# Three projections of batch 1, from the first pass to the stretch ahead of it

## Chip, cores and metric

The kernel runs on one core of a Trainium2 chip. The metric is the device time in microseconds (us) of one execution. Before the change it is 773.31 us, the median of three runs (773.23, 773.31, 774.62).

## What is computed

A transformer block on x of shape (4, 512, 512): four batches, 512 positions, width 512; 32 query heads and 8 key and value heads of 16 features, hidden width 1376.

```
x = x + attention(layernorm(x), Wq, Wk, Wv, Wo)
x = x + ffn(layernorm(x), W_gate, W_up, W_down)
# attention
q, k, v = h @ Wq, h @ Wk, h @ Wv
q = q * cos + rotate_half(q) * sin
k = k * cos + rotate_half(k) * sin
att = where(causal, q @ k.T / sqrt(16), -inf)
out = (softmax(att) @ v) @ Wo
# ffn
(silu(h @ W_gate.T) * (h @ W_up.T)) @ W_down.T
```

## The kernel before

The program has two phases. `phase_1` does the attention of all batches up to the weighted values and the output projection of batch 0; `phase_2` does the rest. The change is in `phase_1` alone.

**The stretch in front.** TensorE transposes the normalised x of batch 0 (four units), makes its key projection (R0), its four query projections (R1 to R4) and its values (V, U), and transposes x of batch 1 (T0 to T3). A unit is a result of one PSUM bank. An R or V unit is 12 matmuls of 512 columns: four chunks of the contraction times three products of high and low parts; they are issued in four pieces of three (`project`, L1124). Then come the scores of groups 0 and 1 of batch 0. A group is one key head with its four query heads. Its scores fill 11 banks of `ps_s` (three in rotation), and VectorE takes the row maximum of each bank (`row_max`: L921 for groups 0 and 1, L916 after). ScalarE and VectorE split the maxima of group 0 in two, TensorE transposes them (`transposed_max`, L1190), ScalarE copies the result to `m_t` (L776), and SyncE stages it as two more rows of `q_rows`.

**The passes.** Four passes (`iteration(b)`, b = 0 to 3) of 8 groups with 4 slots each, 32 slots. In a slot of group n TensorE makes transposed scores of n (`ps_t`, L1206), scores of n + 2 (L1172) and weighted values of n or n - 1 (`ps_o`, L1219). ScalarE takes the exponential (L786), GpSimd masks it (`mask_probs`, L685 and L687), VectorE takes the maxima of group n + 2. At the start of each group GpSimd splits the maxima of the next one (`split_max`, L676 and L678), and TensorE transposes them after the fourth score of the group.

**The projections of the next batch** lie between these. A pass has 40 gaps, five to a group, at the places (slot, head) (0,1), (0,3), (1,3), (2,1), (2,3). `QKV_UNITS` gives each unit's first gap; R and V take one piece in each of four gaps, U and T all four pieces in one:

```
QKV_UNITS = [("R", 0, 0), ("R", 1, 5), ("R", 2, 10), ("R", 3, 15), ("R", 4, 20), ("V", 0, 25), ("U", 0, 30)]
NEXT_T = [("T", 0, 32), ("T", 1, 34), ("T", 2, 36), ("T", 3, 38)]
ROPE_SLOT = [3, 4, 5, 6, 7, 8, 11, 11, 12, 12, 13, 14, 16, 17, 19, 20, 21, 22, 23, 24]
LO_SLOT = {7: 0, 14: 1, 15: 2, 22: 3, 25: 4}
```

All of a pass's units use the one bank `ps_d`. ScalarE copies R units out to `raw` (`raw_rows`, L737; for keys also two half copies, L723 and L724). GpSimd turns them by position in 20 steps (`rotate`, L589; a remainder, L593, in five of them, each followed by `rotated_low`, L604), step s in slot `ROPE_SLOT[s]`. ScalarE takes the top parts (`rotated_top`, L747), and SyncE writes the parts to memory (`store_rotated`) one slot after `LO_SLOT`. T units are transposes of the batch after next (L1113); ScalarE and VectorE (`xt_low`, L895) read them. VectorE also does the layer norm of that batch in passes 0 and 1 (`STATS_AT`, `APPLY_AT`). Pass 2 has no T units; in pass 3 the W units are the output projection of batch 0, and its T units transpose batch 0 for the second phase (`last_xt`).

## Time and profile before

| | |
|---|---|
| median of three runs | 773.31 us |
| profiled execution | 775.21 us |
| its span, first to last instruction | 773.5 us |
| TensorE busy | 742.8 us, 96% |
| VectorE busy | 433.9 us, 56% |
| ScalarE busy | 334.7 us, 43% |
| GpSimd busy | 240.8 us, 31% |
| TensorE's mean granted clock | 0.987 of full speed |

Times inside the execution are counted from the span's start. Busy time is the union of an engine's instructions; a matmul's record also covers its way through the array, so the start-to-start distance of two neighbours is what one costs in a stream. A granted clock of 1.00 is 2.4 GHz, 0.50 is 1.2 GHz. The row ends with the idle time in front of an instruction, and with what ended it.

### The profile page before, as it was taken

Reading aid. Unit: us, or ns where it says so; the run is one execution under the profiler, and the core shown is the slowest. Engines: PE = TensorE matmul, PEld = TensorE weight load, DVE = VectorE, ACT = ScalarE, POOL = GpSimd, SP = SyncE. Lnnn points to the kernel's source line nnn. Section 1 sums busy time; section 2 is a strip of 40 time slices with the busy share of each in tenths; the row PEclk is TensorE's granted clock in tenths of the full one; section 3 lists DMA queues with packets and bytes.
Section 4 is the critical chain, followed back from the end, with each engine's and each line's share of the span. In section 5 each row is a group of like instructions: output and inputs, shape, how many; then the busy total and the mean of one; then the engine's idle time right before and its main releaser. Section 6 shows DMA issues by size and latency. Waiting matters only on the chain.

```text
span 773.5 us, 12217 instructions
## 1 busy us (share of the span) xinstructions
PE 742.8 (96%) x4180; PEld 505.5 (65%) x4180; DVE 433.9 (56%) x1120; ACT 334.7 (43%) x646; POOL 240.8 (31%) x467
## 2 busy tenths in 40 slices
PE   5899999999999999998999999999999999999998
PEld 4645444554454543443788888888888888788886
DVE  6898788887877778997354443233232233231212
ACT  3337767766876788677343222111121111121111
POOL 4157785678557874555000000000000000000000
PEclk9869999999999999999999999999999999999999
DMA  7337677233434454530592102311004020020001
GB/s 271 97 108 254 216 250 228 66 100 111 120 94 126 149 171 148 165 98 36 168 311 69 42 14 107 94 59 54 15 35 156 27 81 27 0 108 1 1 0 55
DMA packets 74759, 81.86 MB, mean 106 GB/s; under 512 B 8864, under 2 KB 58528, under 8 KB 74496
## 3 DMA queue, kind: packets, MB, share of 16 engines
q1 hardware_dynamic: 73408, 79.98, 32.5%
q10 hardware_dynamic: 1296, 1.18, 0.5%
q8 instruction: 30, 0.49, 0.3%
q14 instruction: 25, 0.20, 0.1%
HBM read 57.02 MB, written 33.36 MB: 117 GB/s over the span
## 4 chain that ended last, share of the span: by engine, by line
PE 51%; DVE 0%; issue 0%; DVEq 0%
PE bank L1562 35%; PE ps_y L1614 15%; PE bank L1601 1%; DVE x_in L1544 0%; DVEq L1543 0%
## 5 line engine op out<-in xcount | busy, mean ns | idle before, releaser
L916 DVE CUSTOM_DVE_ANT_0 ps_s<-ps_s,mask_row 128x512 f32<-128x512 f32 (+1 forms) x360 | 192.8, 583 | 50.8 <-PE ps_s L1172 48.0
L786 ACT ACTIVATE probs<-ps_t 128x512 f32<-128x512 f32 (+1 forms) x352 | 179.3, 559 | 70.0 <-PE ps_t L1206 69.9
L1519 DVE TENSOR_TENSOR h<-h,bank 128x512 f32<-128x512 f32 (+1 forms) x44 | 30.2, 687 | 217.2 <-PE bank L1562 217.2
L1172 PE MATMUL ps_s<-k_rows,q_rows 96*128 96x256 bf16 (+3 forms) x512 | 140.5, 309 | 3.5 <-DVE m_raw L916 1.5
L1206 PE MATMUL ps_t<-q_rows,k_rows 98*128 98x512 bf16 (+1 forms) x352 | 127.1, 365 | 3.4 <-ACT probs L786 2.1
L238 POOL TENSOR_TENSOR var_eps<-mean_var,eps 128x1 f32<-128x1 f32 x16 | 3.0, 189 | 282.5 <-DVE mean_var L233 282.5
L1457 ACT ACTIVATE h<-bank 128x512 f32<-128x512 f32 (+1 forms) x44 | 26.3, 598 | 147.5 <-PE bank L1562 147.5
L687 POOL TENSOR_SCALAR_AFFINE_SELECT probs<-probs 128x512 f32<-128x512 f32 x128 | 83.2, 650 | 0.0
L1463 ACT CAST h_hi<-h 128x512 fp32r<-128x512 f32 (+1 forms) x44 | 27.3, 620 | 128.4 <-DVE h L1519 128.4
L1219 PE MATMUL ps_o<-probs,v_ones 128*32 128x512 f32 (+3 forms) x1024 | 82.0, 439 | 0.2 <-ACT o_sb L796 0.2
L1172 PEld LDWEIGHTS ps_s<-k_rows,q_rows 96*128 96x128 bf16 x512 | 49.3, 100 | 43.1 <-DVE m_raw L916 13.8
L1206 PEld LDWEIGHTS ps_t<-q_rows,k_rows 98*128 98x128 bf16 x352 | 34.3, 98 | 52.9 <-issue 20.7
L1614 PE MATMUL ps_y<-wd_hi,h_hi 128*128 128x512 f32 (+1 forms) x176 | 68.8, 391 | 0.0
L1614 PE MATMUL ps_y<-wd_lo,h_hi 128*128 128x512 f32 (+1 forms) x176 | 68.6, 390 | 0.0
L1614 PE MATMUL ps_y<-wd_hi,h_lo 128*128 128x512 f32 (+1 forms) x176 | 68.6, 390 | 0.0
L685 POOL TENSOR_TENSOR carrier<-half 128x1 f32<-128x1 f32 x128 | 26.9, 210 | 95.8 <-ACT probs L786 95.6
L1219 PEld LDWEIGHTS ps_o<-probs,v_ones 128*32 128x32 f32 x1024 | 27.0, 109 | 42.7 <-issue 32.9
L916 DVE DVE_READ_ACCUMULATOR2_ANT m_raw<- 128x1 f32 x360 | 50.5, 140 | 0.0
L1562 PE MATMUL bank<-xt_hi,wg_hi 128*128 128x512 f32 (+1 forms) x128 | 50.0, 390 | 0.0
L1562 PE MATMUL bank<-xt_hi,wg_lo 128*128 128x512 f32 (+1 forms) x128 | 49.9, 390 | 0.0
L1562 PE MATMUL bank<-xt_hi,wu_lo 128*128 128x512 f32 (+1 forms) x128 | 49.9, 390 | 0.0
L1562 PE MATMUL bank<-xt_lo,wg_hi 128*128 128x512 f32 (+1 forms) x128 | 49.9, 390 | 0.0
(161 smaller groups left out, 1370.8 us busy)
## 6 DMA issues: line engine op xcount, KB each, us to landing
scratch_o<-o_sb SPq DMA_DIRECT2D x31, 256.0 KB, 2.1
q_rows<-scratch_q_parts SPq DMA_DIRECT2D x32, 192.0 KB
x_in<-in_x SPq DMA_DIRECT2D x16, 256.0 KB, 4.5
q_rows<-scratch_q_parts SPq DMA_DIRECT2D x32, 128.0 KB
o_in<-scratch_o SPq DMA_DIRECT2D x64, 64.0 KB
inverse<-scratch_inverse SPq DMA_DIRECT2D x64, 64.0 KB
x_res<-in_x SPq DMA_DIRECT2D x16, 256.0 KB, 2.8
out<-x_in SPq DMA_DIRECT2D x16, 256.0 KB, 2.0
```

What stands on the lines that cost most here:

```text
L685: nc.gpsimd.tensor_tensor(carrier[:, g % 2, c:c + 1], half[:, 0:1], half[:, 0:1], ALU.add)
L687: nc.gpsimd.affine_select(out=diagonal, in_=diagonal, compare_op=ALU.is_ge, fill=0.0, base=0, pattern=[[0, GROUP], [1, P]], channel_multip ...
L786: nc.scalar.activation(probs[:, g % 2, heads * u:heads * (u + 1), CHUNK_AT[c]:CHUNK_AT[c + 1]], ps_t[:, pos % S_BANKS, 0:heads * CHUNK_N[c ...
L916: taken = nc.vector.tensor_tensor_reduce(out=head, in0=head, in1=mask_row[:, T - width:T], scale=1.0, scalar=LOWEST, op0=ALU.add, op1=ALU. ...
L1172: mm = nc.tensor.matmul(bank[:, place], q_rows[r][0:ROWS, j, P * q:P * (q + 1)], k_rows[r][0:ROWS, 0:width], start=(place == 0), stop=(mas ...
L1206: nc.tensor.matmul(ps_t[:, pos % S_BANKS, 0:heads * width], k_rows[r][:, P * c:P * (c + 1)], q_rows[r][:, heads * u:heads * (u + 1), P * c:T],
L1219: mm = nc.tensor.matmul(ps_o[32 * j:32 * j + 2 * DH, P * c:T], v_ones[:, c, g % NKV, :], probs[:, g % 2, j, CHUNK_AT[c]:CHUNK_AT[c + 1]], ...
L1457: nc.scalar.activation(h[0:m, r], bank[units["gate", f] % BANKS][0:m, :], ACT.Silu).then_inc(silu_done, 1)
L1463: nc.scalar.copy(h_parts[0][0:m, r], h[0:m, r]).then_inc(h_hi_ready, 1)
L1519: nc.vector.tensor_tensor(h[0:m, r], h[0:m, r], bank[units["up", f] % BANKS][0:m, :], ALU.mult).then_inc(h_ready, 1)
L1562: mm = nc.tensor.matmul(out, weights(w, c), moving(m, c), start=(c == 0 and n == 0), stop=(c == chunks - 1 and n == 2))
L1614: mm = nc.tensor.matmul(ps_y[:, t], h_parts[w][0:m, r, P * t:P * (t + 1)], wd[p][0:m, f, :], start=(f == 0 and k == 0), stop=(f == FT - 1 ...
```

## The change

- Units R0, R1 and R2 of batch 1 (`AHEAD` = 3) leave pass 0. Their 12 pieces stand between the scores of groups 0 and 1 (`AHEAD_AT`: group, slot, head, to unit and piece), R0 into `ps_t`, R1 into `ps_d`, R2 into `ps_o`. The transposed maximum of group 0 goes to a bank of `ps_t` and has semaphores of its own.
- ScalarE copies R0 out ahead of `rotated_top(0, 4)` and of the first maximum, and R1 and R2 behind the last store of batch 0. GpSimd does rotation steps 0 to 2 of batch 1 ahead of pass 0.
- Pass 0 has R3, R4, V and U at gaps 5, 12, 18 and 23; its rotation steps 3 to 19 stand in slots 0 to 19 (`FIRST_ROPE`), and its stores in slots 3, 8, 11, 18 and 22.
- In passes 1 and 2 R2 to U start one gap earlier. In passes 0 and 1 T0 does too. In `ROPE_SLOT` of these passes steps 8 and 11, both with a remainder, no longer share group 3's slots (12 to 15); `MEAN_SLOT` is 15, so that GpSimd's part of the layer norm stands in slot 16, which is group 4's.
- In pass 3 units T1 to T3 go to the three banks of `ps_s` and no longer to `ps_d`.

The declaration of the two new semaphores (`first_max_ready`, `first_max_evacuated`) and unchanged lines are left out:

```diff
@@ -70,29 +70,37 @@
-QKV_UNITS = [("R", 0, 0), ("R", 1, 5), ("R", 2, 10), ("R", 3, 15), ("R", 4, 20), ("V", 0, 25), ("U", 0, 30)]
-NEXT_T = [("T", 0, 32), ("T", 1, 34), ("T", 2, 36), ("T", 3, 38)]
+QKV_UNITS = [("R", 0, 0), ("R", 1, 5), ("R", 2, 9), ("R", 3, 14), ("R", 4, 19), ("V", 0, 24), ("U", 0, 29)]
+NEXT_T = [("T", 0, 31), ("T", 1, 34), ("T", 2, 36), ("T", 3, 38)]
...
               ("T", 3, 39)]
-UNITS_IN = [QKV_UNITS + NEXT_T] * (B - 2) + [QKV_UNITS, LAST_UNITS]
-PRE_DENSE = KC + N_ROPE + 2 + KC
-PRE_UNITS = PRE_DENSE + 1
...
+AHEAD = 3
+AHEAD_AT = {(0, 1, 1): (0, 0), (0, 1, 3): (0, 1), (0, 2, 1): (0, 2), (0, 2, 3): (0, 3),
+            (1, 0, 1): (1, 0), (1, 0, 3): (1, 1), (1, 1, 1): (1, 2), (1, 1, 3): (1, 3),
+            (1, 2, 1): (2, 0), (1, 2, 3): (2, 1), (1, 3, 1): (2, 2), (1, 3, 3): (2, 3)}
+FIRST_UNITS = [("R", 3, 5), ("R", 4, 12), ("V", 0, 18), ("U", 0, 23)]
+UNITS_IN = [FIRST_UNITS + NEXT_T] + [QKV_UNITS + NEXT_T] * (B - 3) + [QKV_UNITS, LAST_UNITS]
+PRE_DENSE = KC + N_ROPE + 2 + KC + AHEAD
 PRE_BANKS = 1 + S_BANKS
-UNIT0 = [PRE_UNITS + sum(len(u) for u in UNITS_IN[:b]) for b in range(B)]
...
-ROPE_SLOT = [3, 4, 5, 6, 7, 8, 11, 11, 12, 12, 13, 14, 16, 17, 19, 20, 21, 22, 23, 24]
+UNIT0 = [PRE_DENSE + sum(len(u) for u in UNITS_IN[:b]) for b in range(B)]
...
+ROPE_AHEAD = 3
+FIRST_ROPE = [None] * ROPE_AHEAD + [0, 1, 2, 3, 4, 5, 6, 7, 8, 9, 10, 13, 14, 15, 17, 18, 19]
+ROPE_SLOT = [FIRST_ROPE] + [[3, 4, 5, 6, 7, 8, 10, 10, 11, 12, 13, 14, 15, 17, 18, 19, 21, 22, 23, 25]] * (B - 2)
...
 PRE_STEPS = PAIR_STEPS
-LO_SLOT = {7: 0, 14: 1, 15: 2, 22: 3, 25: 4}
-NEXT_XT = {26: 0, 27: 1, 29: 2, 31: 3}
+LO_SLOT = [{2: 0, 7: 1, 10: 2, 17: 3, 21: 4}] + [{7: 0, 13: 1, 16: 2, 23: 3, 27: 4}] * (B - 2)
+NEXT_XT = {25: 0, 27: 1, 29: 2, 31: 3}
...
-X_SLOT, MEAN_SLOT = 26, 14
+X_SLOT, MEAN_SLOT = 26, 15
@@ -305,10 +313,16 @@
+        LAST_UNIT0 = UNIT0[B - 1]
...
-            if isinstance(unit, int) and unit < PRE_DENSE and unit % PRE_BANKS:
+            if unit == PRE_DENSE - 1:
+                return ps_o[:]
+            if unit < PRE_DENSE and unit % PRE_BANKS:
                 return ps_t[:, unit % PRE_BANKS - 1]
+            if unit > LAST_UNIT0 + TT:
+                return ps_s[:, unit - LAST_UNIT0 - TT - 1]
@@ -374,9 +389,17 @@
+        def v_unit(b):
...
+            return UNIT0[b - 1] + len(UNITS_IN[b - 1]) - KC - 1 if 0 < b < B - 1 else UNIT0[b] - 1 if b else KC + N_ROPE + 1
...
-            return UNIT0[b - 1] + k if b else KC + k
+            if b == 0:
+                return KC + k
+            if b == 1:
+                return PRE_DENSE - AHEAD + k
+            return UNIT0[b - 1] + k
@@ -453,7 +476,7 @@
                 if n == 0:
-                    sp.wait_ge(dense_evacuated, PRE_UNITS)
+                    sp.wait_ge(first_max_evacuated, 1)
@@ -513,8 +536,8 @@
                         load_x(b + 3)
-                    if has_next and slot - 1 in LO_SLOT:
-                        store_rotated(sp, b + 1, LO_SLOT[slot - 1])
+                    if has_next and slot - 1 in LO_SLOT[b]:
+                        store_rotated(sp, b + 1, LO_SLOT[b][slot - 1])
@@ -668,6 +691,8 @@
                     rotated_low(0, REST_STEP.index(s))
+            for s in range(ROPE_AHEAD):
+                rotate(1, s)
@@ -700,7 +725,7 @@
                     if has_next:
-                        for s, at in enumerate(ROPE_SLOT):
+                        for s, at in enumerate(ROPE_SLOT[b]):
@@ -772,8 +797,8 @@
                 if n == 0:
-                    act.wait_ge(dense_ready, PRE_UNITS)
-                    nc.scalar.copy(m_t[0][:], ps_d[rows, 0:P]).then_inc(dense_evacuated, 1)
+                    act.wait_ge(first_max_ready, 1)
+                    nc.scalar.copy(m_t[0][:], ps_t[rows, 0, 0:P]).then_inc(first_max_evacuated, 1)
@@ -821,14 +846,14 @@
                         if g == 0:
-                            v_place(b, UNIT0[b - 1] + 6 if b else KC + N_ROPE + 1)
+                            v_place(b, v_unit(b))
...
                                 dense_read(b, *done[slot, j])
-                    if has_next and slot in LO_SLOT:
-                        rotated_top(b + 1, LO_SLOT[slot])
+                    if has_next and slot in LO_SLOT[b]:
+                        rotated_top(b + 1, LO_SLOT[b][slot])
@@ -864,10 +889,13 @@
             store_rotated(act, 0, 3)
+            raw_rows(1, 0, r_unit(1, 0))
...
             store_rotated(act, 0, 4)
+            for k in range(1, AHEAD):
+                raw_rows(1, k, r_unit(1, k))
@@ -983,7 +1011,7 @@
                     if slot in NEXT_XT:
-                        work.append(lambda: xt_low(b + 2, NEXT_XT[slot], UNIT0[b] + len(QKV_UNITS) + NEXT_XT[slot]))
+                        work.append(lambda: xt_low(b + 2, NEXT_XT[slot], UNIT0[b + 1] - KC + NEXT_XT[slot]))
@@ -1102,6 +1130,9 @@
+                if piece == 0 and unit > LAST_UNIT0 + TT:
+                    pe.wait_ge(max_done, BANKS_OF * GROUPS)
+                    return
@@ -1182,8 +1213,8 @@
                 if n == 0:
-                    bank_free(PRE_UNITS - 1, 0)
-                    to, ready = ps_d[:], dense_ready
+                    pe.wait_ge(dense_evacuated, KC + N_ROPE + 2 + KC)
+                    to, ready = ps_t[:, 0], first_max_ready
@@ -1199,6 +1230,8 @@
                 pos = T_AT[c] + u
+                if n == 0 and c == 0 and j == 0:
+                    pe.wait_ge(dense_evacuated, PRE_DENSE - AHEAD + 1)
@@ -1211,7 +1244,9 @@
                 if c == 0:
-                    if positive(n):
+                    if n == 0:
+                        pe.wait_ge(dense_evacuated, PRE_DENSE)
+                    else:
@@ -1251,7 +1286,7 @@
                         mm.then_inc(dense_ready, 1)
-            for unit in range(KC, PRE_DENSE):
+            for unit in range(KC, PRE_DENSE - AHEAD):
@@ -1263,6 +1298,9 @@
                         scores(0, n, i, j)
+                        if (n, i, j) in AHEAD_AT:
+                            k, piece = AHEAD_AT[n, i, j]
+                            dense(1, "R", k, r_unit(1, k), piece)
```

TensorE's queue at the end of group 1's first slot, before. `ps_s` holds scores, `m_parts` the split maxima of group 0; the row with 384 columns opens the second slot.

```order
113 L1172 MATMUL ps_s<-k_rows,q_rows 128x512
114 L1179 MATMUL ps_s<-mask_q,ident_b 128x128
115 L1190 MATMUL ps_d<-ident_b,m_parts 128x128
116 L1172 MATMUL ps_s<-k_rows,q_rows 128x384
117 L1179 MATMUL ps_s<-mask_q,ident_b 128x128
118 L1172 MATMUL ps_s<-k_rows,q_rows 128x384
```

And with the change (`xt`, `w`: parts of batch 1's x and of the weights):

```order
126 L1203 MATMUL ps_s<-k_rows,q_rows 128x512
127 L1210 MATMUL ps_s<-mask_q,ident_b 128x128
128 L1203 MATMUL ps_s<-k_rows,q_rows 128x512
129 L1210 MATMUL ps_s<-mask_q,ident_b 128x128
130 L1155 MATMUL ps_d<-xt_hi,w_hi 128x512
131 L1155 MATMUL ps_d<-xt_lo,w_hi 128x512
132 L1155 MATMUL ps_d<-xt_hi,w_lo 128x512
133 L1221 MATMUL ps_t<-ident_b,m_parts 128x128
134 L1203 MATMUL ps_s<-k_rows,q_rows 128x384
135 L1210 MATMUL ps_s<-mask_q,ident_b 128x128
```

Two pieces of R1 stand in this slot, one of them just ahead of the transposed maximum, which now goes to `ps_t`. The other ten pieces stand in the same way behind each second score from group 0's second slot on.

ScalarE's queue from the last `rotated_top` of batch 0 to the first exponentials, before:

```order
24 L747 COPY r_top<-rot 128x1024
25 L767 CAST m_parts<-m_raw 128x16
26 L776 CAST m_t<-ps_d 32x128
27 L403 DMA scratch_q_parts<-r_top 16x8x512 x2
28 L403 DMA scratch_q_parts<-r_low 16x8x512
29 L786 ACTIVATE probs<-ps_t 128x512 x4
```

And with the change:

```order
24 L748 ACTIVATE raw<-ps_t 64x512
25 L749 COPY raw<-ps_t 64x512
26 L762 COPY raw<-ps_t 128x512
27 L772 COPY r_top<-rot 128x1024
28 L792 CAST m_parts<-m_raw 128x16
29 L801 CAST m_t<-ps_t 32x128
30 L426 DMA scratch_q_parts<-r_top 16x8x512 x2
31 L426 DMA scratch_q_parts<-r_low 16x8x512
32 L762 COPY raw<-ps_d 128x512
33 L762 COPY raw<-ps_o 128x512
34 L811 ACTIVATE probs<-ps_t 128x512 x4
```

Three copies of R0 (`raw<-ps_t`) now precede the last `r_top` and the first maximum (`m_parts`, `m_t`), and two copies, of R1 and R2, precede the first exponentials of pass 0.

GpSimd's queue in pass 0, from the first split of maxima to the fourth mask, before (`carrier` and AFFINE_SELECT are one mask; `rot` and `turned` are rotation steps):

```order
35 L676 CAST m_parts<-m_raw 128x16
36 L678 TENSOR_TENSOR m_parts<-m_raw,m_parts 128x16
37 L685 TENSOR_TENSOR carrier<-half 128x1
38 L687 AFFINE_SELECT probs<-probs 128x4x128
39 L685 TENSOR_TENSOR carrier<-half 128x1
40 L687 AFFINE_SELECT probs<-probs 128x4x128
41 L685 TENSOR_TENSOR carrier<-half 128x1
42 L687 AFFINE_SELECT probs<-probs 128x4x128
43 L589 TENSOR_TENSOR rot<-raw,cos 128x512
44 L685 TENSOR_TENSOR carrier<-half 128x1
45 L687 AFFINE_SELECT probs<-probs 128x4x128
```

And with the change:

```order
38 L701 CAST m_parts<-m_raw 128x16
39 L703 TENSOR_TENSOR m_parts<-m_raw,m_parts 128x16
40 L616 TENSOR_TENSOR rot<-rot 128x512
41 L627 TENSOR_TENSOR r_low<-rot 128x512
42 L710 TENSOR_TENSOR carrier<-half 128x1
43 L712 AFFINE_SELECT probs<-probs 128x4x128
44 L612 TENSOR_TENSOR rot<-raw,cos 128x512
45 L710 TENSOR_TENSOR carrier<-half 128x1
46 L712 AFFINE_SELECT probs<-probs 128x4x128
47 L612 TENSOR_TENSOR rot<-raw,sin 128x512
48 L710 TENSOR_TENSOR carrier<-half 128x1
49 L712 AFFINE_SELECT probs<-probs 128x4x128
```

Before, one rotation step stands ahead of the fourth mask and none ahead of the first three. Now three steps and an `r_low` stand among the first three masks, and one more step and the fourth mask follow the last row shown.

## Rows read from the trace of the kernel before

**Rows 1.** Stretch, length, busy us (x) of PE, PEld, DVE, ACT, POOL; PEclk; DMA, GB/s.

```profile
40.50:53.60 13.10, 12.11 (x56) 5.45 (x57) 12.44 (x23) 2.46 (x4) 7.52 (x7) 0.63 0.42 122
57.04:137.55 80.51, 77.72 (x565) 39.57 (x565) 65.41 (x217) 59.76 (x121) 57.48 (x107) 1.00 0.71 230
370.76:773.50 402.74, 399.58 (x1776) 327.96 (x1776) 132.71 (x216) 82.64 (x140) 8.87 (x24) 1.00 0.21 68
```

**Rows 2.** The same view, from one transposed maximum to the next.

```profile
57.00:66.30 9.30, 9.30 (x58) 4.79 (x57) 7.27 (x26) 7.32 (x15) 4.79 (x12) 1.00 0.75 269
66.30:76.50 10.20, 10.20 (x75) 5.23 (x75) 8.49 (x28) 7.64 (x15) 10.04 (x16) 1.00 0.65 224
76.50:87.30 10.80, 10.21 (x75) 5.25 (x75) 8.43 (x28) 6.71 (x14) 6.76 (x14) 1.00 0.70 229
87.30:98.00 10.70, 10.29 (x74) 5.18 (x73) 8.09 (x31) 8.48 (x16) 10.38 (x19) 1.00 0.82 240
98.00:108.20 10.20, 10.16 (x74) 5.24 (x75) 7.71 (x26) 6.71 (x14) 8.47 (x14) 1.00 0.73 253
108.20:117.30 9.10, 9.10 (x72) 4.67 (x72) 8.24 (x26) 7.16 (x15) 8.42 (x16) 1.00 0.65 195
117.30:127.90 10.60, 9.19 (x75) 4.57 (x74) 8.48 (x28) 8.43 (x18) 5.18 (x12) 1.00 0.87 264
127.90:137.60 9.70, 9.36 (x74) 4.70 (x72) 8.80 (x30) 7.31 (x16) 3.45 (x11) 1.00 0.50 155
...
168.00:179.40 11.40, 10.36 (x74) 5.20 (x73) 8.10 (x31) 8.53 (x16) 11.08 (x19) 1.00 0.27 83
...
287.70:295.70 8.00, 7.86 (x63) 3.13 (x62) 6.96 (x26) 5.84 (x14) 3.43 (x10) 1.00 0.65 188
```

**Rows 3.** The same view, cut where TensorE's clock changed.

```profile
43.00:47.40 4.40, 4.40 (x22) 2.11 (x21) 4.24 (x9) 0.65 (x2) 4.16 (x5) 0.50 0.40 117
47.40:50.80 3.40, 2.47 (x15) 0.75 (x13) 3.24 (x7) 1.35 (x3) 1.01 (x1) 1.00 0.12 35
50.80:54.20 3.40, 3.35 (x17) 1.85 (x16) 3.24 (x7) 0.00 (x0) 0.00 (x0) 0.50 0.69 203
```

**Rows 4.** Neighbouring projection matmuls in the timeline, slow and full clock.

```profile
14.25 0.63 PE L1124 MATMUL ps_d<-xt_hi,w_lo 128*128 128x512 f32 x1
14.68 0.63 PE L1124 MATMUL ps_d<-xt_hi,w_hi 128*128 128x512 f32 x1
...
27.42 0.39 PE L1124 MATMUL ps_d<-xt_lo,w_hi 128*128 128x512 f32 x1
27.64 0.39 PE L1124 MATMUL ps_d<-xt_hi,w_lo 128*128 128x512 f32 x1
```

**Rows 5.** Timeline: TensorE's first transposed score, the start of pass 0.

```profile
53.59 0.63 PE L1206 MATMUL ps_t<-q_rows,k_rows 98*128 98x512 bf16 x1
```

**Rows 6.** Timeline, ScalarE: last top part, first maximum, a copy of `raw`.

```profile
47.33 1.04 ACT L747 COPY r_top<-rot 128x1024 bf16<-128x1024 bf16 x1 [3.75 <-POOL rot L593]
48.28 0.21 ACT L767 CAST m_parts<-m_raw 128x16 bf16<-128x16 f32 x1
60.59 0.59 ACT L723 ACTIVATE raw<-ps_d 64x512 f32<-64x512 f32 x1 [0.26 <-PE ps_d L1124]
```

**Rows 7.** Timeline, GpSimd: a rotation step, then, one mask later, a remainder.

```profile
68.12 1.28 POOL L589 TENSOR_TENSOR rot<-rot,turned 128x512 f32<-128x512 f32 x1
...
70.10 1.04 POOL L593 TENSOR_TENSOR rot<-rot 128x512 f32<-128x512 f32 x1
```

**Rows 8.** Timeline, TensorE: the waits for a transfer, GpSimd and the bank.

```profile
84.14 0.39 PE L1206 MATMUL ps_t<-q_rows,k_rows 98*128 98x512 bf16 x1 [0.59 <-DMA q_rows<-m_t]
...
122.82 0.63 PE L1113 MATMUL ps_d<-ident,xn 128*128 128x128 f32 x4 [1.16 <-DVE xt_lo L895]
...
179.44 0.23 PE L1190 MATMUL ps_t<-ident_b,m_parts 128*128 128x128 bf16 x1 [1.08 <-POOL m_parts L678]
...
365.74 0.63 PE L1113 MATMUL ps_d<-ident,xn 128*128 128x128 f32 x4 [1.17 <-DVE xt_lo L895]
```

3 lines of the change are left out of this document (2 added, 1 removed).

## Prediction

> **What bounds the kernel now.** I read the time by stages first, then the same view cut from one transposed maximum to the next, then where the clock changes, then the timeline and the order of the queues. The second phase keeps TensorE busy for 399.6 of 402.7 us [rows 1]; the change does not touch it. In pass 0 TensorE is busy for 77.7 of 80.5 us, the other engines for 57 to 65. In the stretch before it, from 40.5 to 53.6, VectorE is the full engine (12.4 of 13.1 us, 23 instructions, 0.54 each), and TensorE has a mean clock of 0.63 only. So projections leave a stretch that TensorE bounds for one that VectorE bounds. The questions are how much room there is, at which clock, and what bounds pass 0 when TensorE has less to do.
>
> **Price of a piece.** Projection matmuls follow each other by 0.22 to 0.23 us at full clock (27.42, 27.64) and by 0.43 at half clock (14.25, 14.68) [rows 4]. A piece of three is 0.68 or 1.28 us. Twelve pieces move: 8.2 or 15.3 us. The Trainium skill, in "TensorE: Matmul & The Clock Gate", section "Back-to-back issue gap", gives about 131 ns for a 512-column matmul in a stream with weight loads. By that the 36 matmuls would be 4.7 us instead of 8.2, and about 3.5 less would be moved; the rows disagree with it, and nothing below uses it.
>
> **Ahead of pass 0** (the cost). I follow the queue from the sixth bank of scores, done at about 43.6, since everything before it is unchanged. The clock is at half until 47.4 [rows 3]; I keep that.
> - To 47.4: two pieces of R0 (2.6) and most of three banks of scores (0.43 each). Then at full clock the rest of that bank, one more, and two pieces: R0 is done at 49.4.
> - ScalarE now copies R0 out first, three copies of 0.6 [rows 6], to 51.2. Behind them wait the last `r_top` (1.04, at 47.33 before) and the first maximum (at 48.28 before), which ends at 52.5 (another 0.21). VectorE stands still for about 1.6 us behind that maximum, since its low part is next in its queue; TensorE for about 0.9. The transposed maximum is out at 53.2.
> - VectorE has ten banks left, at about 0.55 each: to 58.3. TensorE has seven banks of scores (4608 columns, 1.9 us), six pieces (4.1) and 0.7 of waiting for banks: the first transposed score comes at 59.9, where it was at 53.59 [rows 5].
> - ScalarE copies R2 (0.6) before the first exponential, which TensorE meets three banks on: 0.9. On the other side the two pieces of R0 are gone from the first slot (1.36), and the clock is full, where 0.6 us were at half (0.2 saved).
> So the transposed maximum at 57.04 [rows 1] moves to about 62.0: **+5.0 us**. Bounds: with every piece at half clock and nothing hidden it is 15.3 less 1.6, so +13.7; with full clock from 43.6 on it is 3.8/2 less, and without VectorE's standstill 0.9 less, so +2.2. I take the replay, because the clock was in fact granted at 47.4, and TensorE now has more to do in that time, not less.
>
> **Pass 0** (the gain). Two windows give a rule. Four pieces in a group: 10.2 us (the second of rows 2). None: 8.0 (287.7 to 295.7). Four pieces are 2.7 us, so TensorE's own floor is 7.4 and another limit is 8.0; there VectorE is busy for 6.96. With layer norm or `xt_low` beside it VectorE is busy for 8.2 to 8.8 in 9.1 to 9.7 us. GpSimd's prices: a step 1.25, a mask 0.73 (what is left from 68.12 to 70.10) [rows 7], a remainder 1.1 and a low part 1.0 (its duration is 1.04 too), and as estimates a split 0.47 (two instructions of the size of the 0.21 in rows 6) and the layer norm's part 1.2. Group by group, now against after:
> - 0: 9.3; two pieces fewer give 7.9, but GpSimd gets three more steps and a low part (4.9 of busy time become 9.3, of which it did idle 1.1 late in the group): 8.2.
> - 1: 10.2; two pieces, 8.8; GpSimd has 9.35: 9.35.
> - 2 and 3: 10.8 and 10.7; still four pieces: 10.2 each. The transfer of the maxima came 0.59 late at 84.14 [rows 8], and GpSimd, full for 10.38 of 10.7, becomes lighter by a step and a low part.
> - 4: 10.2; no piece but U: GpSimd with 9.3 (layer norm, two steps, remainder, low part) is the limit: 9.3.
> - 5: 9.1 to 8.8; T0 is here instead of two pieces and U, and VectorE has 8.2.
> - 6: 10.6 to 9.3; the wait of 1.16 for `ps_d` at 122.82 [rows 8] goes, as T0 is a gap earlier.
> - 7: 9.7 to 9.6.
> Sum 74.95 against 80.5: **-5.6 us**. Bounds: -8.2 - 1.2 + 1.36, so -8.0, if only TensorE counted; -2.3 if groups 0 and 1 take GpSimd's 10.0 of the window at 66.3 and the others VectorE's 9.7.
>
> **Other queues in pass 0.** SyncE has six writes of the keys in slot 3, then six row loads, then the staging of the next maximum; before, this stood in slots 8 and 9 and cost the 0.59 at 84.14. I expect the same wait one or two groups earlier: nothing gained or lost. GpSimd's three early steps (3.8 us) lie beside its idle stretch ahead of pass 0 (7.5 of 13.1 busy), at no cost.
>
> **Passes 1 and 2.** Group 1 gets a fifth piece in each (+0.65), group 5 one fewer (in pass 1 T0 takes its place). In pass 1 the wait of 1.16 at T0 goes (the same place as 122.82), and so does the 1.08 at 179.44 [rows 8]: there GpSimd is busy for 11.08 of 11.4 us [rows 2], and without one low part (1.0) and the layer norm (1.2) it has 9.0 beside TensorE's 10.2. Pass 1: **-1.6**. Pass 2: 0, as group 5 gives back what group 1 takes.
>
> **Pass 3.** T3 waits 1.17 for `ps_d` at 365.74 [rows 8], with only two groups' tails behind it: last transposed score, exponential, mask, weighted values, copy. In a bank of its own it waits no longer; ScalarE is free at 365.5 for the next exponential: **-1.0** (bounds 0 and -1.2).
>
> **Sum.** +5.0 - 5.6 - 1.6 + 0 - 1.0 = -3.2 us. It is made against the span of 773.5; the same difference off the median of 773.31 gives **770.1 us** (the profiled execution itself took 775.21, 1.9 above the median). A difference of less than 0.2%, 1.55 us, is about what a measurement of this kernel cannot tell from none.
>
> **The rivals.**
> 1. *The front is cheap.* The clock is granted sooner, since TensorE no longer has holes between banks. For it: at 43.0 to 47.4 TensorE is already busy throughout [rows 3]. Against: it was so at half clock for over 3 us without a grant. At +2.5 instead of +5.0, and with 1 us more from pass 0: 766.6.
> 2. *Pass 0 is held by another engine.* GpSimd takes 10.0 in groups 0 and 1, VectorE 9.7 elsewhere, as in the lower bound above: -2.3 instead of -5.6. Then the sum is +0.1: 773.4, no change. For it: VectorE at 8.8 of 9.7 us in the eighth window of rows 2, and GpSimd's 10.04 in the second. Against: the 9.1 us window with two layer norm steps shows that VectorE can take 8.2 in 9.1.
> 3. *The front is at half clock.* At 50.8 the clock fell, after 3.4 us in which TensorE was busy for 2.47 only [rows 3]. With VectorE standing still and TensorE following it bank by bank, the clock falls again or is not granted at 47.4. Each us at half clock costs 0.5. The change loses its gain when half clock lasts 6.4 us beyond 47.4. From 47.4 to the end of the stretch TensorE has 12.5 us of work less waits of about 1.6, so nearly 11 us at full clock would be 22 at half: +11, of which waits for VectorE and ScalarE hide about 3. That gives +13.0 in front and a time of about 778. For it: rows 3, where half clock holds from 50.8 to 54.2 with TensorE busy for 3.35 of 3.4 us. Against: pieces fill just those holes. The Trainium skill's "TensorE: Matmul & The Clock Gate", section "A second HAM failure mode: psum-queue depth-cycling", describes this: short idle times between groups of matmuls that cycle through banks make the clock go up and down. By it the time would be that of this rival or between it and the forecast; the fall at 50.8 agrees with it.
>
> **How the numbers follow.** Forecast 0.49 (768.3 to 771.7), rival 1 0.14, rival 2 0.22, rival 3 with its milder forms 0.15. Rival 2 lies within 0.2% in most of its chance; of the forecast's upper edge and rival 3's mild forms a little does too. Faster by over 0.2% (under 771.76): 0.62. Within 0.2%: 0.23. Slower (over 774.86): 0.15. The range leaves out the faster half of rival 1 (under 766.0) and most of the slower cases: 766.0 to 775.5.
>
> **What would show it.** First transposed score near 60 and the transposed maximum after it near 62; TensorE's clock at full from 47.4 without another fall; the first maximum on ScalarE at 52 behind three copies and `r_top`. Pass 0 of about 75 us with groups 0, 1 and 4 at 8.2 to 9.4, GpSimd busy nearly all of groups 1 and 4, and no wait at T0 of passes 0 and 1; group 3 of pass 1 at 10.3; no wait for T3 at the end. A pass 0 of 78 us speaks for rival 2; half clock after 51 for rival 3; a first transposed score before 57.5 for rival 1. The forecast is wrong if the second phase changes its length, since nothing here prices that.

## The result and the profile after

The changed kernel takes 780.83 us, the median of four runs (779.23 to 784.76), against 773.51 for the kernel before on the same chip: a ratio of 1.0094, with a 95% interval from 1.0074 to 1.0114. It is slower by 7.3 us. The forecast said 770.1, faster; its range, 766.0 to 775.5, does not hold the result. In a second set eleven runs of the change gave 778.19 (775.33 to 782.0) against 774.45, a ratio of 1.0044 [1.0026, 1.0063]. So the loss is 4 to 7 us, and both intervals lie above 1.

The profiled execution took 779.23 us, its span is 777.5, against 773.5 before: 4.0 us to explain. I cut it as the forecast did. This is the view by stretches of the changed kernel (columns as in [rows 1]): from the sixth bank of scores to the first transposed score, pass 0, and the second phase.

```profile
40.50:62.06 21.56, 19.16 (x90) 11.25 (x92) 14.60 (x24) 4.71 (x8) 11.61 (x10) 0.82 0.29 82
64.02:143.61 79.59, 71.29 (x528) 34.26 (x535) 65.92 (x221) 57.01 (x118) 52.65 (x103) 1.00 0.73 232
376.30:777.50 401.20, 398.06 (x1776) 326.64 (x1776) 132.81 (x216) 82.45 (x140) 8.91 (x24) 1.00 0.21 68
```

The second row is the one to look at. TensorE's work in pass 0 fell from 77.7 us [rows 1] to 71.3, as the 36 matmuls are gone. The pass fell by 0.9 only: TensorE, which had 2.8 us of idle time in it, now has 8.3. The work left the pass, and idle time took its place.

| stretch | before | after | difference | forecast |
|---|---|---|---|---|
| to the transposed maximum that starts pass 0 | 57.04 | 64.02 | +6.98 | +5.0 |
| pass 0 | 80.51 | 79.59 | -0.92 | -5.6 |
| pass 1 | 81.48 | 80.20 | -1.28 | -1.6 |
| pass 2 | 76.63 | 77.57 | +0.94 | 0 |
| pass 3, from its first group on | 58.67 | 58.68 | 0.0 | 0 |
| last transposed maximum to the second phase | 16.43 | 16.24 | -0.2 | -1.0 |
| second phase | 402.74 | 401.20 | -1.5 | 0 |

**The groups of pass 0**, from one transposed maximum to the next, groups 0 to 7 (as [rows 2] before):

```profile
64.02:73.66 9.64, 8.70 (x52) 3.59 (x52) 8.33 (x31) 7.24 (x15) 8.09 (x15) 1.00 0.58 199
73.66:82.90 9.24, 8.83 (x66) 4.19 (x68) 7.12 (x24) 7.13 (x15) 9.08 (x16) 1.00 1.02 331
82.90:93.13 10.23, 10.08 (x72) 5.13 (x74) 8.49 (x28) 7.04 (x15) 7.83 (x14) 1.00 0.78 243
93.13:103.85 10.72, 10.30 (x74) 5.00 (x73) 8.28 (x32) 7.08 (x15) 8.97 (x16) 1.00 0.85 280
103.85:113.89 10.04, 7.93 (x65) 3.77 (x66) 9.52 (x28) 7.81 (x16) 8.23 (x16) 1.00 0.58 171
113.89:122.34 8.45, 7.86 (x64) 3.78 (x66) 7.40 (x26) 6.48 (x14) 3.52 (x10) 1.00 0.67 222
122.34:133.92 11.58, 8.38 (x70) 4.13 (x69) 7.99 (x28) 6.90 (x16) 3.49 (x10) 1.00 1.00 297
133.92:143.61 9.69, 9.20 (x73) 4.67 (x71) 8.79 (x30) 7.34 (x16) 3.45 (x10) 1.00 0.32 101
```

Groups 0, 4 and 6 stand out: in each TensorE is idle for about 1 to 3 us, and in group 4 neither TensorE (7.93) nor GpSimd (8.23) fills the time, but VectorE has 9.52 of 10.04. TensorE's own waits, in the timeline of the changed kernel, name what ended each:

```profile
53.06 0.23 PE L1221 MATMUL ps_t<-ident_b,m_parts 128*128 128x128 bf16 x1 [1.20 <-DVE m_parts L956]
...
73.66 0.23 PE L1221 MATMUL ps_t<-ident_b,m_parts 128*128 128x128 bf16 x1 [0.41 <-POOL m_parts L703]
...
113.89 0.23 PE L1221 MATMUL ps_t<-ident_b,m_parts 128*128 128x128 bf16 x1 [1.04 <-POOL m_parts L703]
...
131.73 0.39 PE L1239 MATMUL ps_t<-q_rows,k_rows 98*128 98x512 bf16 x1 [2.71 <-DMA q_rows<-m_t]
...
372.08 0.64 PE L1254 MATMUL ps_o<-probs,v_ones 128*32 128x512 f32 x4 [1.11 <-POOL probs L712]
```

**In front**, the queues of the other engines explain the first of them. ScalarE, VectorE and GpSimd in the timeline of the changed kernel:

```profile
48.88 0.59 ACT L748 ACTIVATE raw<-ps_t 64x512 f32<-64x512 f32 x1 [5.06 <-PE ps_t L1155]
49.50 0.58 ACT L749 COPY raw<-ps_t 64x512 f32<-64x512 f32 x1
50.10 0.59 ACT L762 COPY raw<-ps_t 128x512 f32<-128x512 f32 x1
50.59 1.05 ACT L772 COPY r_top<-rot 128x1024 bf16<-128x1024 bf16 x1
51.53 0.22 ACT L792 CAST m_parts<-m_raw 128x16 bf16<-128x16 f32 x1
...
51.79 1.22 DVE L956 TENSOR_TENSOR m_parts<-m_raw,m_parts 128x16 bf16<-128x16 f32 x1 [1.22 <-ACT m_parts L792]
...
51.71 1.26 POOL L612 TENSOR_TENSOR rot<-raw,cos 128x512 f32<-128x512 f32 x1 [3.02 <-ACT r_top L772]
```

The first maximum on ScalarE (51.53) stands behind R0's three copies and `r_top`, as foreseen. What was not foreseen is VectorE's low part of it: 16 columns wide, 0.18 us before the change (at 48.52), 1.22 now. It starts at 51.79 and ends at 53.01; GpSimd's first early rotation step runs from 51.71 to 52.97. The Trainium skill, in "SBUF — State Buffer", section "SBUF: two separate sides", says that a VectorE instruction with two operands in SBUF and a GpSimd instruction share a pair of ports that one holds for its whole length. The trace agrees: the small instruction ends 0.04 us behind the large one.

**The clock**, same view, cut where it changed in front:

```profile
45.00:51.90 6.90, 6.81 (x39) 4.06 (x39) 4.04 (x8) 2.82 (x5) 3.65 (x5) 1.00 0.20 57
51.90:53.60 1.70, 0.23 (x1) 0.10 (x1) 1.70 (x3) 0.26 (x1) 1.62 (x2) 1.00 0.00 0
53.60:55.60 2.00, 1.74 (x9) 0.92 (x10) 2.00 (x5) 0.00 (x0) 1.92 (x2) 0.91 0.35 97
55.60:58.60 3.00, 3.00 (x12) 1.99 (x11) 1.38 (x4) 0.59 (x1) 0.08 (x1) 0.50 0.73 207
```

Full speed came 2.4 us sooner than before (45.0, not 47.4 [rows 3]); behind the idle stretch of 51.9 to 53.6 the clock fell to 1.2 GHz for 3 us. The second phase is 1.5 us shorter for a like reason, which belongs to the execution and not to the change. Before, it ran at a mean of 0.52 from 371.50 to 374.80; now it does not. In the eighteen profiled executions of this document the time from the last transposed maximum to the end is either 417.3 to 417.4 us (the change's first profile) or 419.0 to 419.2 (the kernel before, and the change's second profile). First before, then after:

```profile
371.50:374.80 3.30, 3.30 (x9) 2.51 (x8) 0.82 (x2) 0.62 (x1) 0.00 (x0) 0.52 0.67 196
```

```profile
377.00:380.30 3.30, 3.30 (x17) 2.70 (x16) 0.82 (x2) 0.62 (x1) 0.00 (x0) 1.00 0.70 196
```

**The copies.** SyncE's queue ahead of the wait at 131.73, in the timeline of the changed kernel:

```profile
120.99 1.19 SPq L451 DMA_DIRECT2D scratch_wd_raw<-in_wd  x2
122.22 0.77 SPq L469 DMA_DIRECT2D k_rows<-scratch_k_parts  x1
...
125.34 0.42 SPq L472 DMA_DIRECT2D q_rows<-scratch_q_parts  x1
125.81 0.67 SPq L482 DMA_DIRECT2D q_rows<-m_t  x1
```

The 8 KB of maxima are issued at 125.81 and TensorE has them at 131.73, 5.9 us on. Ahead of them stand two copies of 688 KB, from memory to memory, of weights that only the second phase needs (twelve of these lie in pass 0, `copy_raw`), and six row loads. The DMA engines are full in that group (share 1.00); they are so in group 1 too (1.02), where no wait followed, so the share alone does not tell.

That the two copies go out together is the change's own doing. SyncE's queue at the same place before the change:

```profile
111.93 0.57 SPq L428 DMA_DIRECT2D scratch_wd_raw<-in_wd  x1
114.52 1.23 SPq L403 DMA_DIRECT2D scratch_q_parts<-r_top  x2
...
116.43 1.00 SPq L428 DMA_DIRECT2D scratch_wd_raw<-in_wd  x1
...
120.90 0.67 SPq L459 DMA_DIRECT2D q_rows<-m_t  x1
```

There the store of slot 23 stood between the two copies of group 5. The change puts it in slot 22, ahead of both: SyncE waits for its data until 117.70, and then both copies go out at 120.99, 4.8 us ahead of the maxima.

### The profile page after: what moved, and what is told of

Read it like the earlier page. It is cut to its first block, busy times and chain, and to the rows that moved or that the text cites. A ratio compares the mean times of both kernels' runs of the same rounds, so it can differ in the third digit from the quotient of the medians.

```text
span 777.5 us, 12187 instructions
## 1 busy us (share of the span) xinstructions
PE 738.6 (95%) x4149; PEld 503.6 (65%) x4180; DVE 434.9 (56%) x1120; ACT 333.1 (43%) x646; POOL 241.9 (31%) x467
## 4 chain that ended last, share of the span: by engine, by line
PE 51%; DVE 0%; issue 0%; DVEq 0%
PE bank L1600 35%; PE ps_y L1652 15%; PE bank L1639 1%; DVE x_in L1582 0%; DVEq L1581 0%
## 5 line engine op out<-in xcount | busy, mean ns | idle before, releaser
L1203 PEld LDWEIGHTS ps_s<-k_rows,q_rows 96*128 96x128 bf16 x512 | 47.3, 99 | 47.0 <-DVE m_raw L944 22.0
L1600 PE MATMUL bank<-xt_lo,wu_hi 128*128 128x512 f32 (+1 forms) x128 | 49.9, 390 | 0.0
```

Of the source, the lines that this page charges most:

```text
L1203: mm = nc.tensor.matmul(bank[:, place], q_rows[r][0:ROWS, j, P * q:P * (q + 1)], k_rows[r][0:ROWS, 0:width], start=(place == 0), stop=(mas ...
L1600: mm = nc.tensor.matmul(out, weights(w, c), moving(m, c), start=(c == 0 and n == 0), stop=(c == chunks - 1 and n == 2))
```

## The experiments

Sixteen kernels in four sets, each timed beside the kernel before on the same chip. Two single times (of e8 and e13) at nearly twice that of their neighbours are left out of ranges and ratios; they move a median by 0.04 at most. In the tables "start" is the time of the transposed maximum that begins pass 0, and ratios are to the kernel before, with the 95% interval. Starts and passes come from one profiled execution each, so read the start with the scatter of the clock in mind: the change itself has 64.0, 62.9 (the second set), and 61.2, 61.5 and 61.6 in three kernels with the same front (e11, e4, e13). In the profiled executions the clock came back to full speed in front at 40 to 47.5 us, and in some it fell again behind the first maximum.

### First set: the parts of the change

**The rest of the change without the move** (`e1_rest_alone`): kernel before, plus

```diff
-QKV_UNITS = [("R", 0, 0), ("R", 1, 5), ("R", 2, 10), ("R", 3, 15), ("R", 4, 20), ("V", 0, 25), ("U", 0, 30)]
+QKV_UNITS = [("R", 0, 0), ("R", 1, 5), ("R", 2, 9), ("R", 3, 14), ("R", 4, 19), ("V", 0, 24), ("U", 0, 29)]
...
+            if unit > UNIT0[B - 1] + TT:
+                return ps_s[:, unit - UNIT0[B - 1] - TT - 1]
```

and with it the new rotation, store and mean slots.

> The kernel before with everything of the change except the move: R0 to R2 stay in pass 0, but the units of passes 0 to 2 start a gap earlier, T0 at gap 31, the new slots of rotation steps and stores, and T1 to T3 of pass 3 in ps_s. Theory A (the whole loss comes from the move: front and pass 0): from the trace after, pass 1 gained 1.3 us and pass 2 lost 0.9, pass 3 nothing, so the time is within 1.5 us of the kernel before, 772 to 774. Theory B (the later passes carry a loss of their own, by the fifth piece of group 1, 1.2 us in each): 775 or more.

**The maximum first on ScalarE** (`e2_max_first`): the change, with

```diff
-            raw_rows(1, 0, r_unit(1, 0))
             rotated_top(0, 4)
             first_max_high()
+            raw_rows(1, 0, r_unit(1, 0))
```

> The change, but ScalarE does the last top part of batch 0 and the first maximum ahead of the three copies of R0. Theory A (the front is late because the first maximum stands behind R0's copies and then meets GpSimd's first rotation step): VectorE's m_parts takes 0.2 and not 1.2 us, the first transposed maximum comes near 51.5 instead of 53.1 and the one of group 1 near 62 instead of 64.0, 1.5 to 2.5 us faster than the change if the clock does not fall. Theory B (TensorE's twelve pieces set the length of the front, whatever the order): the one of group 1 stays within 0.5 us of 64.0.

**GpSimd's early steps behind the split** (`e3_pool_after_split`): the change, with

```diff
+            pool.wait_ge(m_split, 1)
             for s in range(ROPE_AHEAD):
```

> The change, but GpSimd starts the three early rotation steps only when VectorE has split the first maximum. Theory A (GpSimd's step that starts at 51.71 holds up VectorE's two-input instruction of 51.79): m_parts back to 0.2 us, first transposed maximum 1.0 us earlier, at about 52.0 if the clock is granted as in the trace after. Theory B (the 1.2 us have another reason, for instance the waits in the queue): m_parts still about 1.2 us.

**The last two copies in pass 1** (`e4_copies_later`): the change, with

```diff
-                    if not positive(b) and i >= 2 and g < 6:
+                    if not positive(b) and i >= 2 and g < 5:
+                        copy_raw(2 * g + i - 2)
+                    if b == 1 and i >= 2 and g == 5:
                         copy_raw(2 * g + i - 2)
```

> The change, but the last two of the twelve copies of the raw feed-forward weights (688 KB each) are made in pass 1 and not in group 5 of pass 0. Theory A (the staging of the maxima for group 7, issued at 125.81, stood behind these two copies and landed 5.9 us later): the wait of 2.71 us at 131.73 is gone or under 0.5, the distance of the transposed maxima of groups 6 and 7 falls from 11.58 to about 9.3, and the kernel is about 2 us faster than the change. Theory B (SyncE's own lateness is the cause: six row loads ahead): the wait stays above 1.5.

| | median (range) | ratio | start | pass 0 | 1 | 2 |
|---|---|---|---|---|---|---|
| before | 774.59 | | 57.0 | 80.51 | 81.48 | 76.63 |
| e1, no move | 773.62 (771.61 to 776.04) | 0.9988 [0.9971, 1.0005] | 57.5 | 80.73 | 80.29 | 78.16 |
| e2, maximum first | 776.8 (773.18 to 780.1) | 1.0024 [1.0003, 1.0044] | 58.2 | 82.46 | 80.20 | 78.11 |
| e3, GpSimd later | 777.1 (773.31 to 778.75) | 1.0026 [1.0, 1.0053] | 61.1 | 79.79 | | |
| e4, two copies later | 777.83 (774.37 to 778.82) | 1.0041 [1.0024, 1.0057] | 61.5 | 76.93 | 80.61 | 77.62 |

What follows: e1 acquits the rest. It brings pass 1 down by 1.2 and pass 2 up by 1.5, and makes no difference that can be measured. The loss comes with the move and what was done to pass 0 for it. e3 settles the small instruction: with GpSimd held back it takes 0.18 again. VectorE and TensorE in the timeline of e3:

```profile
51.45 0.18 DVE L957 TENSOR_TENSOR m_parts<-m_raw,m_parts 128x16 bf16<-128x16 f32 x1 [1.21 <-ACT m_parts L793]
```

```profile
51.69 0.23 PE L1222 MATMUL ps_t<-ident_b,m_parts 128*128 128x128 bf16 x1 [0.15 <-DVE m_parts L957]
```

TensorE's wait fell from 1.20 to 0.15. In the ratio (1.0026, where the change has 1.0094 and, below, 1.0044) little of that can be told from scatter. e4 removed the wait of 2.7 us altogether (pass 0 at 76.93), and its ratio is 1.0041. e2 made the maximum early, but in its pass 0 the clock fell (0.96 over the pass) and the transfer came 2.67 us late. Each repair works at its place, and none of the three kernels gets under the kernel before, so the next step was to combine them.

### Second set: the change again, two repairs, and the slots

> The change itself once more, beside the variants of this call, so that they can be compared on one chip. Theory A (the time of the change scatters because TensorE's clock is granted and taken back at another point of the front and of pass 0 in each execution): 3 to 9 us slower than the kernel before, with the transposed maximum of group 1 anywhere from 61 to 66 us, and with the distances of the maxima in passes 1 to 3 the same to 0.1 us. Theory B (the 7.3 us of the first comparison are a fixed cost): within 1 us of +7.

`e6_order_copies` is e2 and e4 together.

> The change with both repairs: last top part and first maximum of batch 0 ahead of R0's copies on ScalarE, and the last two raw weight copies in pass 1. If the two losses add: m_parts 0.2 us, the transposed maximum of group 1 at 58 to 61.5, no wait over 1 us for the staged maxima in pass 0, pass 0 at about 77 us; 3 to 5 us faster than the change beside it, within 2 us of the kernel before. If they hide each other: as the better of the two alone.

`e7_slots` is e6 with GpSimd's plan of pass 0 mended and the gaps, slots and stores of pass 2 as before the change:

```diff
-FIRST_ROPE = [None] * ROPE_AHEAD + [0, 1, 2, 3, 4, 5, 6, 7, 8, 9, 10, 13, 14, 15, 17, 18, 19]
+FIRST_ROPE = [None] * ROPE_AHEAD + [0, 1, 2, 3, 4, 5, 6, 7, 8, 9, 10, 13, 14, 15, 16, 17, 20]
-LO_SLOT = [{2: 0, 7: 1, 10: 2, 17: 3, 21: 4}] + ...
+LO_SLOT = [{1: 0, 7: 1, 10: 2, 17: 3, 22: 4}] + ...
```

> As e6_order_copies, and the slots of GpSimd in pass 0 moved: the top part of the keys in slot 1, steps 17 and 18 in slots 16 and 17, step 19 and its low part in slot 20, and pass 2 with the gaps, slots and stores of the kernel before. Theory A (VectorE's normalising instructions of slots 18 and 19 take 1.3 and 1.4 instead of 0.54 us because a rotation step of GpSimd runs beside them; GpSimd is late at the end of group 4; the fifth piece costs pass 2 0.9 us): the two back near 0.54, the distance at group 4 from 10.04 to 9.2 or less, group 0 from 9.65 to 9.3 or less, pass 2 from 77.6 back to 76.6; 1.5 to 2.5 us faster than e6_order_copies. Theory B (group 4 is bound by something else): 10.0 stays.

`e8_pieces_left_out` is the change without 35 of the 36 matmuls in front: of units R0 to R2 of batch 1 only the last product is computed, so queries and keys of that batch are incomplete.

```diff
+                    if ahead and not (c == KC - 1 and n == 2):
+                        continue
```

> The change with 35 of the 36 matmuls ahead of pass 0 left out: of R0, R1 and R2 of batch 1 only the last product is computed, so keys and the first two query parts of batch 1 are wrong; everything behind them on the other engines stays. It measures what the pieces themselves cost in front. Theory A (they are paid nearly in full, since the room beside VectorE is at half clock): first transposed score at 54 to 55.5 instead of 59 to 62, 5 us or more off the change. Theory B (the order on ScalarE and the wait of VectorE make the front long, the pieces hide in it): first transposed score at 57 or later.

| | median (range) | ratio | start | pass 0 | 1 | 2 |
|---|---|---|---|---|---|---|
| before | 774.45 | | | | | |
| e5, the change | 778.19 (775.33 to 782.0) | 1.0044 [1.0026, 1.0063] | 62.9 | 80.77 | 80.25 | 78.01 |
| e6, order and two copies | 774.97 (772.68 to 776.94) | 1.0009 [0.9994, 1.0024] | 58.8 | 78.47 | 80.25 | 77.97 |
| e7, and slots | 772.62 (769.87 to 776.8) | 0.9978 [0.9962, 0.9995] | 58.7 | 78.93 | 80.81 | 76.25 |
| e8, no pieces in front | 775.11 (771.85 to 776.48) | 1.0001 [0.9983, 1.0019] | 58.8 | 80.1 | | |

e8 is the plainest statement on the change: with 35 matmuls not done at all it is still no faster than the kernel before. Leaving them out takes 3.1 us off the median. The rest is the queues and what the clock makes of them: in e8's trace TensorE waits 1.56 for VectorE's low part of the first maximum, and then runs at 1.2 GHz from about 51 to 57.5, and the maxima come 1.87 late at 127.06. e7 is the first kernel below the one before, and its group 4 takes 8.12 instead of 10.04. But its pass 0 is no shorter than e6's: two waits for the maxima's transfer, 1.77 at 76.54 and 2.03 at 116.91, and a fall of the clock behind the first (group 2 takes 11.58 at a mean of 0.87) had taken the place of what the slots won.

### Third set: the copies, and a control

`e9_all_copies_later` is e7 with all twelve copies in pass 1:

```diff
-                    if not positive(b) and i >= 2 and g < 5:
-                        copy_raw(2 * g + i - 2)
-                    if b == 1 and i >= 2 and g == 5:
+                    if b == 1 and i >= 2 and g < 6:
                         copy_raw(2 * g + i - 2)
```

> The kernel with both repairs of ScalarE's order, GpSimd's slots in pass 0 and the old pass 2 (772.62 us, pass 0 78.93) kept its two waits of 1.77 and 2.03 us for the transfer of the maxima, in groups 1 and 5 of pass 0. Now all twelve copies of the second phase's weights stand in pass 1, none in pass 0. Theory A (the 8 KB transfer is late behind the 688 KB copies): both waits fall under 0.6, pass 0 takes 75.5 to 76.5 and the time is 770 to 771. Theory B (it is late behind the stores of the keys and the row loads, which are a slot earlier here): the waits stay over 1.5, and the time is 772.6 again. Pass 1, whose DMA share was half that of pass 0, should stay at 80.2 to 80.8; if it grows by over 1 us, the copies only took the waits along.

`e10_repairs_no_move` is e1 with the same edit and pass 2 as before.

> The control for the kernel beside it: the projections stay in pass 0, and it has the rest of the change, the old pass 2 and all twelve copies in pass 1. Theory A (moving the projections is worth something once order and slots are right): 771.8 to 773, at least 1 us above the kernel with the move; from 774.5: pass 1 -1.2, the end -0.2, the wait of 0.6 in pass 0 at most. Theory B (all that is won lies in the repairs): the same as the kernel with the move or below it. Front as before (57.0 to 57.5), pass 0 80 to 80.5, pass 1 80.3, pass 2 76.6.

`e11_slots_alone` is the change with e7's two lines of slots.

> The change with GpSimd's plan of pass 0 alone repaired (last two steps and the remainder out of the slots of the layer norm's normalising, the keys' top parts a slot earlier); ScalarE's order in front, the copies and pass 2 as in the change, 778.2. Theory A (group 4 of pass 0 was held by GpSimd and by VectorE slowed beside it): group 4 falls from 10.0 to about 8.2, of which the wait for the maxima's transfer behind it takes part back; pass 0 78 to 79, time 776.3 to 777. Theory B (what a group gives the next one takes back): group 4 falls, the pass stays at 79.6 to 80.8 and the time at 778.2.

`e12_before_copies_later` is the kernel before with the edit of the copies.

> The kernel before with all twelve copies in pass 1 and nothing else. Only one wait of 0.59 for the maxima's transfer stood in pass 0 there. Theory A: it goes, 774.0 to 774.4, not to be told from the kernel before. Theory B (the copies also cost pass 0 in ways that show no wait): 773 or less. If pass 1 has less room than its DMA share suggests, it is slower than before, over 775.

| | median (range) | ratio | start | pass 0 | 1 | 2 |
|---|---|---|---|---|---|---|
| before | 774.41 | | | | | |
| e9, all three repairs | 769.4 (768.51 to 771.04) | 0.9941 [0.9927, 0.9956] | 57.7 | 73.88 | 82.40 | 76.77 |
| e10, the control | 772.13 (769.59 to 773.92) | 0.9971 [0.9958, 0.9983] | 56.6 | 79.41 | 81.63 | 76.70 |
| e11, slots alone | 777.6 (775.26 to 780.22) | 1.0037 [1.0022, 1.0051] | 61.2 | 81.55 | 80.18 | 77.48 |
| e12, before, copies later | 774.06 (770.64 to 776.41) | 0.9992 [0.9974, 1.001] | 55.2 | 80.52 | 81.47 | 76.59 |

This set answers the question. Pass 0 of e9, and groups 0, 4 and 6 of it, in the view by stretches:

```profile
57.72:131.60 73.88, 71.09 (x528) 34.01 (x535) 64.06 (x221) 56.76 (x118) 52.78 (x103) 1.00 0.45 136
```

```profile
57.72:66.78 9.06, 8.54 (x52) 3.58 (x52) 7.85 (x30) 7.09 (x15) 8.97 (x15) 1.00 0.52 160
...
96.89:105.01 8.12, 7.77 (x66) 3.78 (x66) 7.12 (x26) 7.32 (x16) 6.30 (x14) 1.00 0.26 82
...
113.12:121.92 8.80, 8.31 (x70) 4.08 (x69) 7.99 (x28) 6.89 (x16) 3.48 (x10) 1.00 0.65 196
```

TensorE's work is what it was in the change (71.09 against 71.29), and the pass is 5.7 us shorter. The move is worth 2.7 us once nothing else in pass 0 is late: e9 against the control, 769.4 against 772.13, with intervals of the ratios that do not touch. In e11 group 4 fell to 8.12, and the pass grew all the same. TensorE's waits in e11:

```profile
79.81 0.61 PE L1239 MATMUL ps_t<-q_rows,k_rows 98*128 98x512 bf16 x1 [2.50 <-DMA q_rows<-m_t]
...
122.03 0.39 PE L1239 MATMUL ps_t<-q_rows,k_rows 98*128 98x512 bf16 x1 [2.24 <-DMA q_rows<-m_t]
```

It is the same wait at two other places. The wait of 2.71 in group 6 is gone (8.80 instead of 11.58) though no copy was moved: the mended slots put the store back between group 5's two copies, which go out at 118.08 and 121.13. But the pairs at 69.06 and 112.04 now stand 5.6 and 4.9 us ahead of a staging for which a shorter group leaves less time, and behind the first wait the clock fell (means of 0.87 and 0.85 in groups 1 and 2). Before the change the copies cost nothing that can be measured: e12 without them in pass 0 has 774.06, as the first theory had it, but keeps its wait of 0.59, at 82.29, so that wait was never theirs, which neither theory had. e9 also shows a first limit: in pass 1 two copies are issued at 179.31, 1.3 us behind a staging at 178.04, and TensorE waits at 182.91. SyncE and TensorE in the timeline of e9:

```profile
178.04 0.74 SPq L484 DMA_DIRECT2D q_rows<-m_t  x1
178.82 0.44 SPq L490 DMA_DIRECT2D scratch_o<-o_sb  x1
179.31 1.22 SPq L453 DMA_DIRECT2D scratch_wd_raw<-in_wd  x2
```

```profile
182.91 0.39 PE L1241 MATMUL ps_t<-q_rows,k_rows 98*128 98x512 bf16 x1 [1.72 <-DMA q_rows<-m_t]
```

Another pair was issued 6.9 us ahead of that staging, at 171.11. The expectation had named a pass 1 longer by over 1 us as the sign that the copies only take their waits along, and in part they do: against e7, pass 0 is 5.05 shorter (waits of 1.8 and 2.0 and 1.0 of clock) and pass 1 1.6 longer.

Over all eighteen traces, where TensorE waited for the maxima, the time from their issue to TensorE's start goes by what was issued ahead. It is 2.0 to 3.3 us where no copy stands within 8 us ahead, and the pair 1.2 us behind adds nothing there (2.91 before the change, 2.98 without copies in e12). It is 3.6 to 4.0 with one copy 4.1 to 4.5 us ahead, and 4.5 to 5.9 with a pair 4.7 to 5.6 ahead. With a pair 6.7 to 7.8 us ahead it is 3.3 to 4.9.

### Fourth set: one repair taken back at a time

`e13_change_all_copies` is the change with e9's edit of the copies.

> The change with all twelve copies of the second phase's weights in pass 1, nothing else. Theory A (three causes that hide each other, of which the late transfer is one): its wait of 2.7 in group 5 goes and none takes its place in pass 0, but group 4 stays at 10.0: pass 0 76.5 to 77.5, time 774.5 to 776 against 778.2 for the change. Theory B (the copies are the cause): 771 to 773.

`e14_old_order` is e9 with ScalarE's order of the change (the edit of e2 undone).

> The repaired version (769.4) with ScalarE's order of the change in front: three copies of R0 ahead of the keys' last top part and the first maximum. Theory A (the order costs a delay of 3 us to the first transposed maximum, an idle stretch on TensorE and a fall of the clock behind it): mark of group 1 at 61 to 63 where it was 57.7, time 772.5 to 774. Theory B (VectorE's row of banks hides it, the front is bound by the clock alone): 769.4 to 770.5.

`e15_old_slots` is e9 with the two lines of e7's diff undone.

> The repaired version with GpSimd's slots of pass 0 as in the change. Theory A: group 4 back at 10.0 from 8.1, and some of it taken back by group 5; pass 0 75.3 to 76, time 770.8 to 771.5. Theory B (GpSimd's late end of group 4 is made up for in the next groups): 769.4 to 770.

`e16_copies_apart` is e9 with the copies one to a group:

```diff
-                    if b == 1 and i >= 2 and g < 6:
-                        copy_raw(2 * g + i - 2)
+                    if b == 1 and i == 2:
+                        copy_raw(g)
+                    if b == 0 and i == 2 and g >= 4:
+                        copy_raw(g + 4)
```

> The repaired version with one copy of 688 KB in the third slot of a group and none behind it: eight in pass 1, four in groups 4 to 7 of pass 0, where it had two back to back in six groups of pass 1. Theory A (two copies back to back, 1.4 MB, are what the 8 KB transfer is late behind): the wait of 1.72 in group 4 of pass 1 falls under 0.6, none over 0.6 comes up in pass 0, pass 1 80.2 to 80.8, pass 0 as it was, 73.9 to 74.2; time 767.7 to 768.5. Theory B (a single copy delays it enough, or the rows' loads do): the wait stays near 1.7 or moves to pass 0; 769.4 or more.

| | median (range) | ratio | start | pass 0 | 1 | 2 |
|---|---|---|---|---|---|---|
| before | 774.7 | | | | | |
| e13, the change, all copies later | 776.71 (772.68 to 778.18) | 1.0024 [1.0007, 1.004] | 61.6 | 79.02 | 81.28 | 77.97 |
| e14, e9 with the old order | 772.0 (770.42 to 773.94) | 0.9968 [0.9956, 0.998] | 60.4 | 73.94 | 80.88 | 76.64 |
| e15, e9 with the old slots | 771.83 (769.94 to 773.81) | 0.9969 [0.9956, 0.9981] | 59.9 | 76.57 | 80.76 | 76.72 |
| e16, e9 with copies apart | 768.37 (765.52 to 769.89) | 0.9923 [0.9903, 0.9943] | 58.6 | 74.32 | 80.26 | 76.44 |

With the two others mended, ScalarE's order costs 2.6 us (772.0 less 769.4), the slots 2.4 (771.83 less 769.4) and ten of the twelve copies 3.2 (e7's 772.62 less 769.4). By the ratios, which set each kernel against the one before on its own chip, they are 2.1, 2.2 and 2.9. With about 1.3 that pass 2 gains by its old plan (77.5 to 78.2 against 76.3 to 76.8) that is 9.5, or 8.5 by ratios, against a distance of 8.8, or 8.0, between the change (778.19) and e9. So the prices nearly add up when they are taken from the mended kernel. Taken from the change (the 778.19 of the second set), the same repairs brought 0.6 (e11), 1.5 (e13) and 1.4 (e2). The intervals allow each of these differences an error of 1.5 to 2 us, so the times alone do not separate the two sums. The traces do: in e11 and e2 a wait that goes is replaced by the next one, or by a fall of the clock. I had expected e13 to show 76.5 to 77.5 for pass 0 and 774.5 to 776 us; it has 79.02 and 776.71, because group 5 takes 10.74 where e15, with the same slots, has 8.25. The view by stretches of that group tells why, e13 first, then e15:

```profile
111.39:122.13 10.74, 10.74 (x65) 4.86 (x66) 7.57 (x26) 6.82 (x14) 3.57 (x10) 0.70 0.27 81
```

```profile
109.72:117.97 8.25, 8.01 (x65) 3.73 (x66) 7.40 (x26) 6.48 (x14) 3.51 (x10) 1.00 0.33 98
```

TensorE's mean clock is 0.70 in e13, at 1.2 GHz from 112 to about 117, behind group 4 with its two waits of 0.85 and 1.04; in e15 the same two waits cost no clock. So a group in which TensorE idles can cost a second time, in some executions.

e14 shows that the order costs time without any fall behind it. The stretch in which TensorE stands still, and what follows it, in e14:

```profile
49.85:51.55 1.70, 0.23 (x1) 0.10 (x1) 1.70 (x3) 0.26 (x1) 1.62 (x2) 1.00 0.00 0
...
52.00:60.40 8.40, 8.20 (x45) 4.76 (x44) 6.05 (x14) 2.31 (x5) 3.11 (x6) 1.00 0.37 107
```

The first row is the change's row of 51.90 to 53.60 to the last digit, 2.05 us earlier. Yet here the clock did not fall behind it, and there it did. The start is 2.7 us later than e9's, but not all of that is the order: in e14 the clock was at half for 6.8 us in front (33.4 to 40.2), in e9 for 3.4 (39.7 to 43.1). Against e2, e6 and e7, whose clock went as in e14 and whose order is e9's (58.2 to 58.8), it is 1.5 to 2.2 later. In the change's profiled execution the fall comes on top: 3 us at half clock, 1.5 at most.

e16 is the fastest here, 6.3 us or 0.8% under the kernel before, though its interval overlaps e9's. Its pass 1 has no wait for the maxima (80.26): one copy stands at 172.48, 6.2 us ahead of the staging (178.68), and one follows at 180.13. With pairs at these places the same wait was 1.72 in e9, 0.58 in e14 and 0.20 in e15, so how long they delay the 8 KB varies. A single copy is not free either: in its pass 0, with one 4.1 us ahead, the maxima come 0.33 late at 112.27, and group 5 takes 8.50 instead of 8.11.

Other expectations that were missed: pass 0 of e6 (78.47 for 77, as its group 5 ran at a mean clock of 0.82), of e11 (81.55 for 78 to 79) and of e15 (76.57 for 75.3 to 76; its time, 771.83, for 770.8 to 771.5); pass 1 of e10 (81.63 for 80.3, with waits of 0.60 and 0.74 for the maxima); e14's start (60.4 for 61 to 63) and time (772.0 for 772.5 to 774). e9 did better than expected (pass 0 73.88 for 75.5 to 76.5, time 769.4 for 770 to 771).

## Why the prediction was wrong

The step that failed is **pass 0**, -5.6 forecast and -0.9 measured. Group by group, forecast, the change, and e9:

| group | 0 | 1 | 2 | 3 | 4 | 5 | 6 | 7 | sum |
|---|---|---|---|---|---|---|---|---|---|
| forecast | 8.2 | 9.35 | 10.2 | 10.2 | 9.3 | 8.8 | 9.3 | 9.6 | 74.95 |
| change | 9.64 | 9.24 | 10.23 | 10.72 | 10.04 | 8.45 | 11.58 | 9.69 | 79.59 |
| e9 | 9.06 | 8.81 | 10.58 | 10.72 | 8.12 | 8.11 | 8.80 | 9.68 | 73.88 |

- *Other queues in pass 0, "nothing gained or lost".* This is the largest error. I priced the transfer of the maxima by the one wait of 0.59 in the trace of before and let it stand. The wait that I looked for, one or two groups earlier, did not come; another did, in group 6. Half of the 4.6 us missing in pass 0 is group 6 (2.3), which is that transfer. The rows had the warning: a DMA share of 0.87 in the group from 117.30 [rows 2], which I was about to shorten by TensorE's wait of 1.16. In e1, where that wait is gone and the projections stay, the maxima are 0.61 late in the same group. And I did not follow SyncE's queue: the store that I moved from slot 23 to slot 22 sent two copies out together, 4.8 us ahead of the staging. I named a floor for TensorE, VectorE and GpSimd in each group, and no arrival time for the transfer. e7 to e9 price the other ten copies: 3.2 us.
- *Group 4, "GpSimd with 9.3 is the limit".* A sum of busy times was the wrong measure. GpSimd has 8.23 busy and waits 0.77 and 0.88 for exponentials. VectorE is the fullest, since its two instructions of layer norm take 1.32 and 1.41 beside GpSimd's steps, and 0.54 each in e9. The last wait, 1.04 at 113.89, is still for GpSimd, whose split stands behind a remainder, a low part and a mask. The mended slots remove both at once, so the share of each is not shown. VectorE in the timeline, the change and then e9:

```profile
107.76 1.32 DVE L918 TENSOR_SCALAR xn<-x_in,mean_var,rstd 128x512 f32<-128x512 f32 x1
...
110.33 1.41 DVE L918 TENSOR_SCALAR xn<-x_in,mean_var,rstd 128x512 f32<-128x512 f32 x1
```

```profile
100.80 0.54 DVE L920 TENSOR_SCALAR xn<-x_in,mean_var,rstd 128x512 f32<-128x512 f32 x1
```

GpSimd has a step at 107.52 and a remainder at 110.42 in the change, and no step beside these two in e9. A sum of busy times per engine cannot show that, since one instruction has more than one length.
- *Group 0.* I subtracted GpSimd's 1.1 us of idle time from its 9.3, as if the steps would fall into it. Rotation step 5 waits for the keys' top part on ScalarE, one slot on. GpSimd in the timeline of the changed kernel:

```profile
69.16 1.27 POOL L612 TENSOR_TENSOR rot<-raw,sin 128x512 f32<-128x512 f32 x1 [1.47 <-ACT r_top L772]
```

With that part a slot earlier the group takes 9.06, GpSimd 8.97 of it: GpSimd's bound without the 1.1. Groups 1, 2, 5 and 7 came within 0.4. Group 3 took 10.72, 0.5 more than forecast, and does so in e9 too: the move gained nothing there.
- *Ahead of pass 0, +5.0.* The size was nearly right: +7.0 in the first profile, and the five executions with this front (61.2 to 64.0) lie about the forecast of 62.0. That is partly luck, since the terms as listed (6.3 to the first transposed score, then +0.9, -1.36 and -0.2) add up to +5.7, and not to +5.0. The queue on ScalarE was right in its order, and its first maximum, forecast to end at 52.5, ended at 51.75. Two things were missed: from there to the transposed maximum the forecast had 0.7 us, and it took 1.5, as VectorE's low part became 1.22 beside GpSimd, whose early steps I had put "at no cost"; and the fall of the clock behind the idle time that this makes. The gain was counted without a fall, and that is rival 3 in its mild form.
- *Passes 1 and 2.* -1.3 for -1.6, and +0.9 for 0. The fifth piece in group 1 of pass 2 costs 1.26 (11.41 against 10.15), not the 0.65 of its matmuls: R2's first piece follows R1's last in the one bank `ps_d` and waits 0.26 for ScalarE's copy, and what the other 0.35 is was not found. Group 5 gives back 0.56. With the old plan pass 2 is 76.3 to 76.8 again (e7, e9).
- *Pass 3, -1.0.* The wait for T3 is gone, and the row at 372.08 above shows its successor, 1.11 for the masked exponentials of the last group. The bound of 0 was the right end.
- *Second phase, 0.* -1.5 by the clock's state at its start. It is a matter of the execution: in the change's second profile the stretch from the last maximum to the end has 419.0, as before the change, and not 417.4. I took a single execution's 402.7 as fixed.

The rivals: rival 2 had the right place (pass 0 held by something other than TensorE, 78 us and more) with the wrong engines and too small a price; rival 3 had a part of the truth. Together they held 0.37. Both were priced as if they came alone, and neither knew the transfer. What the forecast had right is that the move itself wins: e9 takes 5.0 us off, of which the control gives 2.3 to the other edits.

Left open: what makes the clock fall behind an idle stretch in one execution (the change, e13) and not behind the same stretch in another (e14, e15); why the same pair of copies delays the maxima by 1.72 in e9 and 0.20 in e15; and how much of e16's 1.0 over e9 is more than scatter.

## What to carry to other kernels

When work is taken off the bounding engine, write down the next limit of every stretch for every resource, with the queue of transfers among them, and ask which transfers had been hidden by the very time that goes, and what a store moved by one slot sends out together. Then price a repair by taking it out of the mended kernel too: in the broken one, three causes of 2 to 3 us each looked like 0.6 to 1.5. And where an instruction on VectorE was seen longer beside GpSimd, place the two apart; a busy time measured where they happened to be apart is not the price where they meet.

## What the runs showed of the hardware

- An instruction of VectorE on 128x16 elements took 0.18 us alone and 1.22 beside a GpSimd instruction of 1.26; one on 128x512 (layer norm) took 0.54 alone and 0.86 to 1.41 beside a step, also in the kernel before (0.89 at 112.52). Where a GpSimd step had started first, it ended 0.27 to 0.29 behind that step's end. Holding GpSimd back (e3) gave 0.18 again for the small one.
- TensorE had an 8 KB transfer 4.5 to 5.9 us after its issue with two memory-to-memory copies of 688 KB issued 4.7 to 5.6 us ahead of it, 3.6 to 4.0 with one such copy 4.1 to 4.5 ahead, and 2.0 to 3.3 with none within 8 us ahead (times of the cases in which TensorE waited for it). The Trainium skill, in "SBUF — State Buffer", section "Can I just issue two DMAs to hit both halves?", says that all transfers of a kernel share the same 16 DMA engines; that fits the share of 1.00 in group 6 of the change.
- Executions of one kernel differ by 2.5 to 7 us here, and the start of pass 0 moves with the state of the clock in front, which came back to full speed at 40 to 47.5 us. In the fronts of e14 and of the change TensorE was busy for the same 0.23 us of 1.7; e14 kept its clock, and the change lost it 2 us later.
